# Feed-forward with rotated weights: folds two units sooner, waits of the down product by chunk and half

## What is computed

```python
x = fwht(x * SU_ug) / SCALE                       # x: layernorm of the tokens, 256 wide
x_up = x @ W_up.T * (Wscale_ug[:INTER] * SCALE)   # INTER = 1024
x_gate = x @ W_gate.T * (Wscale_ug[INTER:] * SCALE)
x = jax.nn.silu(x_gate) * x_up
x = fwht(x * SU_dp) / SCALE                       # Hadamard transform over 1024
x = x @ W_down.T * (Wscale_dp * SCALE)
```

## Time and profile before

| | us |
|---|---|
| median of 3 runs | 1624.12 |
| the runs | 1625.83, 1620.94, 1624.12 |
| the profiled execution | 1622.73 |
| its span | 1620.9 |
| TensorE busy in the span | 1525.7 |
| first gate matmul to first down matmul | 1334.49 to 1380.28 |

### The profile page before, as it was taken

One profiled execution on the slowest core, in us unless ns is written; L12 is line 12 of the kernel. 1 busy time (PEld: TensorE's weight loads), 2 busy tenths in 40 slices (PEclk: granted clock), 3 DMA queues, 4 the chain that ended last, 5 costly groups with the idle time before them and its releaser, 6 DMA issues. The chain is left out here.

```text
span 1620.9 us, 39525 instructions
## 1 busy us (share of the span) xinstructions
PE 1525.7 (94%) x17104; PEld 1222.2 (75%) x17104; DVE 892.3 (55%) x1624; ACT 658.1 (41%) x955; POOL 691.4 (43%) x506
## 2 busy tenths in 40 slices
PE   6898899999999999878998999999999999898998
PEld 3584688888888877666666888888888778746465
DVE  4950576666656626875546655555565153377212
ACT  3544244444444443552013444444444434244221
POOL 5414664465445100633966643654451026270101
PEclk9999799999999999998998999999999999999999
DMA  8016565654563203214025646545541030152402
GB/s 240 2 25 138 118 153 128 141 119 107 117 153 73 67 27 89 95 74 106 0 58 123 150 106 139 117 93 118 136 91 29 15 108 1 44 205 77 148 23 62
DMA packets 66461, 154.47 MB, mean 95 GB/s; under 512 B 14972, under 2 KB 44220, under 8 KB 65424
## 3 DMA queue, kind: packets, MB, share of 16 engines
q1 hardware_dynamic: 65520, 150.10, 37.0%
q0 software_dynamic: 768, 1.84, 0.4%
HBM read 87.51 MB, written 5.51 MB: 57 GB/s over the span
## 5 line engine op out<-in xcount | busy, mean ns | idle before, releaser
L1624 DVE TENSOR_REDUCE latent_psW<-latent_psW 128x1 f32<-128x500 f32 x654 | 418.2, 682 | 234.5 <-PE latent_psW L1519 234.1
L1602 ACT ACTIVATE latent_w<-latent_psS 125x896 f32<-125x896 f32 x384 | 351.7, 919 | 429.7 <-PE latent_psS L1537 426.1
L1547 PEld LDWEIGHTS latent_psO<-latent_val,latent_w 125*64 125x64 f32 x10752 | 324.1, 138 | 25.5 <-issue 11.9
L1547 PE MATMUL latent_psO<-latent_val,latent_w 125*64 125x65 f32 x10752 | 339.8, 223 | 0.6 <-issue 0.6
L1536 PE MATMUL latent_psS<-latent_qA,latent_kA 128*125 128x448 f32 x768 | 290.8, 379 | 3.9 <-DVE latent_qB L1640 2.4
L1537 PE MATMUL latent_psS<-latent_qB,latent_kB 128*125 128x448 f32 x768 | 283.3, 369 | 0.0
L1519 PE MATMUL latent_psW<-latent_kA,latent_qA 128*128 128x500 f32 x654 | 214.5, 398 | 3.1 <-DMA latent_qA<-latent_qh 2.4
L1536 PEld LDWEIGHTS latent_psS<-latent_qA,latent_kA 128*125 128x125 f32 x768 | 143.8, 187 | 31.2 <-ACT latent_w L1602 4.6
L1537 PEld LDWEIGHTS latent_psS<-latent_qB,latent_kB 128*125 128x125 f32 x768 | 144.0, 188 | 19.8
L1519 PEld LDWEIGHTS latent_psW<-latent_kA,latent_qA 128*128 128x128 f32 x654 | 124.8, 191 | 19.5 <-DVE latent_psW L1624 5.0
L946 POOL TENSOR_TENSOR latent_rawT<-latent_rawT,latent_ropeT 128x1000 f32<-128x1000 f32 x48 | 110.8, 2334 | 34.1 <-DMA latent_rawT<-in_ctx_cols 22.3
(11 more groups left out here) (411 smaller groups left out, 2222.5 us busy)
## 6 DMA issues: line engine op xcount, KB each, us to landing
latent_qA<-latent_qh SPq DMA_DIRECT2D x128, 112.0 KB, 2.5
latent_rawT<-in_ctx_cols SPq DMA_DIRECT2D x32, 375.0 KB, 5.8
latent_rawT<-in_ctx_cols SPq DMA_DIRECT2D x64, 187.5 KB, 6.4
latent_raw<-in_ctx SPq DMA_DIRECT2D x32, 375.0 KB
latent_kA<-latent_high SPq DMA_DIRECT2D x32, 375.0 KB, 4.0
latent_kB<-latent_high SPq DMA_DIRECT2D x32, 375.0 KB, 5.4
latent_kA<-latent_rawT SPq DMA_DIRECT2D x32, 375.0 KB, 6.2
experts_wgu<-in_L_gu SPq DMA_DIRECT2D x8, 1024.0 KB, 15.0
```

The costliest lines, as they stand in the source:

```text
L1547: last = pe.matmul(sums[r:r + 64, c, :], w[t % ROUND][:, queries_of(c, r):queries_of(c, r) + 64], val[b % 2][:, t, :], start=(t == 0 and c ...
L1602: act.activation(w[t % ROUND][:, :].rearrange("p (h n) -> p h n", h=2), psS[0:KP, t % 2, :, 0:GH], ACT.Exp).then_inc(exp_done, 1)
L1624: dve.tensor_reduce(bank[:, THIRD + j:THIRD + j + 1], bank[:, 0:THIRD], mybir.AxisListType.X, ALU.max).then_inc(max_ready, 1)
```

## The change

FIRST_FOLD goes from 7 to 5: folds stand in units 5 to 12, w_high and w_low in units 6 to 13 (the two conditions bound them now at both ends). TensorE no longer waits for all 16 h_low ahead of the down product. In tile 0 it waits ahead of chunk k for unit 2k (the first half of the tokens of that chunk), and ahead of tile 4 for all 16. The waits for fold_ready and w_split stay where they were.

```diff
--- before.py
+++ after.py
@@ -2193,7 +2193,7 @@
         h_high = a.sb("h_high", [128, NF, T], F32R)
         h_low = nc.alloc_sbuf_tensor_at("ffn2_h_low", [128, NF, T], F32R, offset=g.q_at)
         w_high, w_low = (a.sb(f"wd_{n}", [128, NF * C], F32R) for n in ("high", "low"))
-        FIRST_FOLD = 2 * NF - 1 - NF
+        FIRST_FOLD = 2 * NF - 3 - NF
         norm = Norm(nc, a, g)
         ps_u = a.ps("ps_u", [128, 2, 512])
         ps_g = a.ps("ps_g", [128, 2, 512])
@@ -2213,7 +2213,7 @@
             def _(pool):
                 butterflies(pool, Chain(pool, pool_chain), wd[:, :, :], wd2[:, :, :], wd_ready)
                 for n in range(2 * NF):
-                    if n > FIRST_FOLD:
+                    if 0 <= n - FIRST_FOLD - 1 < NF:
                         k = n - FIRST_FOLD - 1
                         pool.wait_ge(w_rounded, k + 1)
                         pool.tensor_tensor(w_low[:, k * C:(k + 1) * C], wd[:, k, :], w_high[:, k * C:(k + 1) * C].bitcast(F32),
@@ -2258,11 +2258,14 @@
                         last.then_inc(done, 1)
                 pe.wait_ge(fold_ready, NF)
                 pe.wait_ge(w_split, NF)
-                pe.wait_ge(h_split, 2 * NF)
                 for t in range(NT):
                     if t >= 2:
                         pe.wait_ge(x_done, t - 1)
                     for k in range(NF):
+                        if t == 0:
+                            pe.wait_ge(h_split, 2 * k + 1)
+                        if t == NT // 2 and k == 0:
+                            pe.wait_ge(h_split, 2 * NF)
                         for x, w in ((h_high, w_high), (h_high, w_low), (h_low, w_high)):
                             last = pe.matmul(ps_d[0:TP, t % 2, 0:C], x[:, k, t * TP:(t + 1) * TP], w[:, k * C:(k + 1) * C],
                                              start=(k == 0 and w is w_high and x is h_high), stop=(k == NF - 1 and x is h_low))
```

## The result

| | before | after |
|---|---|---|
| median | 1621.20 (9 runs) | 1617.54 (9 runs) |
| lowest, highest | 1617.69, 1627.09 | 1615.32, 1622.05 |
| profiled execution, its span | 1622.73, 1620.9 | 1617.54, 1615.7 |
| ratio, 95% interval | | 0.997 [0.9959, 0.9982] |

The kernel is faster by 0.18 to 0.41%, clear of no change. The forecast had its likeliest case (0.53) within 0.3%.

The account below looks back on a forecast made before the run. It took TensorE, busy 94% of the span, as the bound. 3.18 us (idle gap) plus 1.51 (slow clock) minus 0 (new waits) gave 4.7 us off the median 1624.12: 1619.4 us, range 1616.4 to 1622.5.

Parts of the forecast that it names:

- The hole: TensorE's stop between last up and first down matmul, waiting for GpSimd's h_low, goes; first down matmul 3.18 us sooner.
- The clock: Tile 0 of the down product no longer runs at the 1.2 GHz level after a stop; 1.51 us less.
- The new waits: Eight added TensorE waits in tiles 0 and 4 are met on arrival and cost 0; upper bound 0.8 us.
- The moved folds: Folds two units sooner cost the loop nothing; fold 0 at unit 5, last w_low 2.9 us before the down product.
- The last layer, moved as one block: From tile 0 on, the stage and the last layer behind it simply move 4.7 us sooner.
- D: Last layer's stops meet the clock worse, adding four slow stretches of 1.5 us: slower, 1625.4 us; chance 0.03.
- C: Last layer, moved by 4.7 us, loses one slow stretch less: gain 6.2 us, 1617.9 us; chance 0.13.
- A: At the down product's start, stop and slow stretch both go: gain 4.7 us, 1619.4 us; chance 0.60.

Follow-up runs that it names:

- folds only: The kernel before with only the folds moved to units 5 to 12, the wait for all 16 h_low left whole; ratio 1.0011, stage 70.79 us.
- before again: The kernel before, taken a second time with no edit; ratio 1.0002 against before, stage 70.66 us.
- waits only: The kernel before with only the waits split by chunk and half, folds left in units 7 to 14; ratio 1.0006, stage 69.55 us.
- 24 more waits: The kernel after, with the wait ahead of each chunk in tiles 0 to 3 instead of tile 0 alone; ratio 0.9968 against before, stage 66.28 us.

## Why the prediction was wrong in its class and right in its sum

The forecast gave the most weight (0.53) to a time within 0.3% of before; that is the class it chose, against faster (0.44) and slower (0.03). The terms of its sum, each against what was measured:

- *The hole, 3.18 us.* The gap went from 3.38 to 0.20: 3.18. Right, and both parts were needed, as forecast: alone they gave 1.10 (forecast 1.15) and 0.25 (forecast 0.3).
- *The clock, 1.51 us.* Tile 0 went from 4.34 to 2.82. Right, and its cause is shown and not only argued: filling the hole with dummy matmuls gives it back with the hole still there. The Trainium skill ("TensorE: Matmul & The Clock Gate", Part 1) says that the same kernel shows a different number of slow matmuls from run to run. The four profiled executions with an unfilled gap differ in where the slow matmuls lie and hardly in their number: 15 or 16 of them start 0.17 to 0.32 us apart instead of 0.12, from the first matmul of tile 0 on in before and folds only, from the fourth in before again, from the tenth with the waits alone. All four lost 1.5 to 1.6 us in tile 0 (4.34 to 4.41 against 2.82), all five executions with the complete change (after twice, and the three kernels built on it) had 2.82 or 2.83.
- *The new waits, 0.* Right: 24 more of them cost no more than 0.01 us.
- *The moved folds, 0.* The fold at unit 5 and the spare 2.9 us ahead of the down product are as worked out.
- *The last layer, moved as one block.* It took 215.43 us before and 216.19 after. The trace's records of the granted clock have 12.2 us at 0.50 behind the stage before and 15.1 after, so there is more slow time, as D had it, but it costs 0.76 us and not D's four times 1.5. Whether the change has a part in it isn't shown: the other four profiles without the complete change have 12.0 to 15.4 us and take 215.4 to 216.4, the other four with it have 12.5 to 18.2 and take 215.2 to 216.5. C, a stretch less, is not what they show.

So the mechanism and the size of the sum stand: 4.69 us against the first profile of before, 4.37 against the second, whose gate and up product was 0.42 shorter. The failed step is the one from the sum to the classes: "A's 4.7 lies just short of that line, so run scatter decides: of its 0.60 I put 0.28 over and 0.32 under", with the line set by "a measurement of this kernel can tell about 0.3%, 4.9 us, from no change; the three runs before are spread over 4.9 us". The spread of single runs isn't what a comparison of many runs can tell. The interval of the ratio from nine runs each is 0.0023 wide, so from its middle it reaches 0.12%, and a change of 0.29% is seen. I made no measurable change the likeliest outcome while my own sum was over twice what the runs could resolve.

The second error is in the point; it did not decide the class. I put the sum on the median of three runs, 1624.12. The nine runs of before, these three among them, have a median of 1621.20, and the 35, 23 and 23 of the later comparisons 1622.52, 1623.02 and 1622.87. About 1.6 us of the forecast's 1.9 us excess is that base: against 1622.5 the same sum gives 1617.8, against 1621.2 it gives 1616.5. A median of three, out of runs that lie 9.4 us apart in these nine, was a poor anchor. The profiled execution (1622.73) lay nearer, but by luck: it is one run of the same spread.

## What to carry to other kernels

When two waits of an engine end close together, list both with their ends: taking away one wins only the distance to the next (1.10 and 0.25 us here, against 3.18 for both), and the clock's share had not come back at a gap of 2.28 us. A wait ahead of the first use of each piece cost nothing here where it was met in a full stream of matmuls, so waits can be split there. Judge a change of a few microseconds by the length of its stage between two fixed instructions, take before twice to see how far that repeats (0.32 us here), and ask what many runs can resolve before calling it unmeasurable.

## What the runs showed that I had not expected

The part of the program ahead of the stage is the same in all these kernels, and yet the first rotation matmul starts anywhere from 1320.56 (waits only) to 1329.84 us (24 more waits): 9.3 us, twice the change. The windows of that part, for these two kernels, show GpSimd, ScalarE and DVE equally busy to 1.5 us, and TensorE busy 6.2 us more in the late one:

```profile
0.00:1320.60 1320.60, 1251.53 (x15649) 1034.47 (x15655) 771.69 (x1372) 565.31 (x770) 597.37 (x423) 0.98 0.41 99
```

```profile
0.00:1329.80 1329.80, 1257.72 (x15648) 1038.38 (x15654) 770.20 (x1372) 565.51 (x770) 597.13 (x422) 0.98 0.41 98
```

The same matmuls took longer there. The clock of so long a window is 0.98 in both, but the trace's records of the granted clock that it averages have 44.4 us at 0.50 ahead of the first rotation matmul in waits only and 54.6 us in 24 more waits. The 10.2 us more at half speed can cost 5.1 us at most (an estimate from these two figures), so the clock accounts for up to about half of the 9.3 us. The times say the same of whole executions: of the 81 runs of before in the later comparisons, the 15 with the lowest mean granted clock (0.973 to 0.976) average 1626.5 us, the 20 with the highest (0.981 to 0.984) 1620.0. What takes the rest, and why the slow time differs between executions of the same code, stays open. What it means is plain: the profiled spans of kernels that differ only in this stage range over 7.9 us (1613.7 to 1621.6), "waits only" has a span of 1613.9 and yet a time ratio of 1.0006, and a span alone would have ranked it among the fastest.

Also unexpected: a gap of 2.28 us cost as much clock as one of 3.4 us. I had left open that it would cost none. How short a gap must be to leave the clock up was not tried, beyond the 0.58 us of the filled one, which did.
